# A four-layer gated cross-attention block on one core: key halves of the exponentials summed on VectorE ahead of the softmax denominators, and filler products moved

## The reference, cut to what matters

```
# layer 0 (as the attention inside its ffn block) and layer 3: causal, 16 heads of 16
scores = einsum('bhqd,bhkd->bhqk', qh, kh) / sqrt(16); scores = where(tril, scores, min)
attn = softmax(scores, axis=-1);  out = einsum('bhqk,bhkd->bhqd', attn, vh) @ Wout.T
# layer 1 ("latent"): 16 heads of 64, keys and values from the context, no mask
attn = softmax(q_h @ k_b^T);      out = (attn @ context_b) folded with the output weights
# layer 2 ("score attention", in the phase called mid): softmax over scores, times the scores' own rows,
# after a low-rank adapter with a top-8 gate, and before a top-2 router with capacity 64
```

## Time and profile before

| | us |
|---|---|
| median of 3 runs | 1128.38 |
| the 3 runs | 1126.38, 1134.92, 1128.38 |
| the profiled execution, its own time | 1119.47 |
| its span, first to last instruction | 1117.5 |
| mean granted TensorE clock in it | 0.951 of full |

### The profile page before, as it was taken

One profiled execution on the slowest core, in us unless ns is written; L12 is line 12 of the kernel. 1 busy time (PEld: TensorE's weight loads), 2 busy tenths in 40 slices (PEclk: granted clock), 3 DMA queues, 4 the chain that ended last, 5 costly groups with the idle time before them and its releaser, 6 DMA issues. The chain is left out here.

```text
span 1117.5 us, 23219 instructions
## 1 busy us (share of the span) xinstructions
PE 1004.8 (90%) x9278; PEld 821.0 (73%) x9278; DVE 715.8 (64%) x1737; ACT 483.4 (43%) x863; POOL 194.9 (17%) x167
## 2 busy tenths in 40 slices
PE   9979889879998899989899999885798899989998
PEld 5747677757787687878778887674696777778787
DVE  1567778867776675666666666657645677654644
ACT  1447777713334434435243333344342334334443
POOL 4100000020001132444330000033101000133342
PEclk9999999979999999999999999967798999899999
DMA  9500000000001122323000000010100000132232
GB/s 335 198 2 3 2 1 3 2 1 2 2 3 44 55 86 83 105 94 100 8 2 2 2 2 2 1 39 1 38 1 1 3 3 18 35 96 83 93 108 71
DMA packets 17706, 48.27 MB, mean 43 GB/s; under 512 B 3072, under 2 KB 5248, under 8 KB 17472
## 3 DMA queue, kind: packets, MB, share of 16 engines
q1 hardware_dynamic: 17600, 46.80, 12.9%
HBM read 45.61 MB, written 1.05 MB: 42 GB/s over the span
## 5 line engine op out<-in xcount | busy, mean ns | idle before, releaser
L1669 POOL TENSOR_TENSOR p_WML<-p_raw,p_WMH 128x768 fp32r<-128x768 f32 x56 | 103.7, 1852 | 155.5 <-ACT p_WMH L1786 150.0
L1822 ACT ACTIVATE p_AHI<-p_A 128x512 fp32r<-128x512 f32 x62 | 39.1, 631 | 142.0 <-DVE p_A L1909 142.0
L1349 ACT ACTIVATE p_E<-PS 128x768 f32<-128x768 f32 x64 | 51.6, 807 | 86.7 <-PE PS L1206 86.5
L1909 DVE TENSOR_TENSOR p_A<-p_A,PS 128x512 f32<-128x512 f32 x62 | 42.6, 687 | 62.0 <-PE PS L1717 61.1
L1913 DVE TENSOR_TENSOR p_ALO<-p_A,p_AHI 128x512 fp32r<-128x512 f32 x62 | 52.1, 841 | 44.0 <-ACT p_AHI L1822 44.0
L1453 DVE TENSOR_REDUCE p_mx<-PS 128x2 f32<-128x512 f32 x64 | 44.0, 688 | 53.6 <-PE PS L1170 53.4
L745 PE MATMUL PS<-p_FT,p_PTS 128*128 128x128 f32 x512 | 63.8, 278 | 12.0 <-DVE XNS L935 10.7
L745 PEld LDWEIGHTS PS<-p_FT,p_PTS 128*128 128x128 f32 x512 | 60.0, 192 | 17.3 <-DVE p_PTS L976 15.9
L83 PE MATMUL PS<-p_WMH,p_AHI 128*128 128x256 f32 x224 | 62.9, 281 | 1.6 <-DVE p_ALO L1913 1.4
L85 PE MATMUL PS<-p_WMH,p_ALO 128*128 128x256 f32 x224 | 62.6, 279 | 0.0
L84 PE MATMUL PS<-p_WML,p_AHI 128*128 128x256 f32 x224 | 62.6, 279 | 0.0
(11 more groups left out here) (523 smaller groups left out, 3269.9 us busy)
## 6 DMA issues: line engine op xcount, KB each, us to landing
p_raw<-in_moe SPq DMA_DIRECT2D x56, 448.0 KB, 3.3
p_fr<-in_fold SPq DMA_DIRECT2D x16, 480.0 KB, 4.6
p_raw<-in_wpack SPq DMA_DIRECT2D x8, 416.0 KB, 5.8
p_early_raw<-in_moe SPq DMA_DIRECT2D x6, 448.0 KB, 3.3
CP<-in_consts SPq DMA_DIRECT2D x1, 1725.0 KB, 9.1
XS<-in_x SPq DMA_DIRECT2D x1, 1024.0 KB, 14.4
W2R<-in_ffn SPq DMA_DIRECT2D x4, 256.0 KB, 3.4
p_W3R<-in_ffn SPq DMA_DIRECT2D x4, 256.0 KB, 3.3
```

What stands on the lines that cost most here:

```text
L1349: act.activation(E[:, n % 4], PS[:, ST:ST + 2, 0:384], ACT.Exp, scale=scale).then_inc(s["ex"], 1)
L1669: g.tensor_tensor(WML[:, n % RING, :], raw[:, i % RAW, 0:SEL], WMH[:, n % RING, 0:SEL].bitcast(F32), ALU.subtract).then_inc(s["w_lo"], 1)
L1909: v.tensor_tensor(A[:, b, :], A[:, b, :], PS[:, GS_BANK, :], ALU.mult).then_inc(s["ag"], 1)
```

## The change

Three edits.

1. In both small attentions DVE adds the two key halves of the exponentials of queries 128 to 255 (`key_sums(q)`, at odd steps, 512 elements a partition) into a new buffer ES; PE's products with ones take the queries 0 to 127 from E and 128 to 255 from ES, after a new wait on `es`. The products with the values stay.
2. In latent attention the same for all queries of the pairs 1 to 12 (`SUMMED`): two additions of 128x512 a pair on DVE, into HN's memory, and four products with ones instead of eight. The first addition waits for POOL's last use of HN (`mk`); ACT's writes of HN wait for the products of pair 12.
3. Fillers: 8 at the end of the latent phase, 6 in mid after `lora_turned(0)`, and the 16 in mid become 32 and wait for `neg` of half 1 (the negated maxima, which the exponentials need) instead of its second exponential.

```diff
@@ -1007,6 +1007,7 @@
                 E = ph.sb("E", [P, 4, 2, 384])
+                ES = ph.sb("ES", [P, 2, 2, P])
                 identr = ph.sb("identr", [P, P], F32R)
...
@@ -1232,11 +1233,16 @@
                                 lo, hi = (S, S + P) if kt else (0, S)
-                                for part in range(2):
-                                    for r in range(4):
-                                        left = OZ[:, 16 * p:16 * p + 32] if part else VZ[:, 2 * (j % 2) + kt, 4 * o + r, 16 * p:16 * p + 32]
-                                        m = pe.matmul(PS[32 * r:32 * r + 32, ND, part * S + kt * P:part * S + S], left, E[:, (2 * q + r // 2) % 4, r % 2, lo:hi],
-                                                      start=part == 0 and kt == 0 and p == 0, stop=part == 1 and kt == 1 and p == 1, skip_group_check=True)
+                                for r in range(4):
+                                    pe.matmul(PS[32 * r:32 * r + 32, ND, kt * P:S], VZ[:, 2 * (j % 2) + kt, 4 * o + r, 16 * p:16 * p + 32],
+                                              E[:, (2 * q + r // 2) % 4, r % 2, lo:hi], start=kt == 0 and p == 0, stop=False, skip_group_check=True)
+                            for qt in range(2):
+                                if qt:
+                                    pe.wait_ge(s["es"], q + 1)
+                                for r in range(4):
+                                    keys = ES[:, r // 2, r % 2, :] if qt else E[:, (2 * q + r // 2) % 4, r % 2, 0:P]
+                                    m = pe.matmul(PS[32 * r:32 * r + 32, ND, S + qt * P:S + qt * P + P], OZ[:, 16 * p:16 * p + 32], keys,
+                                                  start=False, stop=qt == 1 and p == 1, skip_group_check=True)
                             m.then_inc(s["pv"], 1)
...
@@ -1472,6 +1478,13 @@
 
+                        def key_sums(q):
+                            at = slice(2 * (q % 2), 2 * (q % 2) + 2)
+                            v.wait_ge(s["ex"], 2 * q + 2)
+                            if q:
+                                v.wait_ge(s["pv"], q)
+                            v.tensor_tensor(ES[:, :, :, :], E[:, at, :, P:S], E[:, at, :, S:S + P], ALU.add).then_inc(s["es"], 1)
+
                         def context_lo(u):
...
@@ -1573,6 +1586,8 @@
                                 context((n - 5) // 4)
+                            if n % 2:
+                                key_sums(n // 2)
                             if n % 4 == 2 and n >= 6:
...
@@ -1970,6 +1985,8 @@
                 E = ph.sb("E", [P, 4, 2, 2, S])
+                ES = HN[:, :, :].rearrange("p (a b) s -> p a b s", a=2)
+                SUMMED = range(1, 13)
                 mx = ph.sb("mx", [P, 2, 2, 2, 2])
...
@@ -2080,13 +2097,18 @@
                                 pe.wait_ge(s["tr_lo"], KC)
-                            for part in range(3):
+                            for part in range(2 if q in SUMMED else 3):
                                 o = PS[:, XY, part * S:part * S + S] if part < 2 else PS[:, DEN, 0:S]
                                 for kt in range(2):
                                     for i in range(4):
                                         left = CTN[:, 2 * j + kt, 32 * part:32 * part + 32] if part < 2 else ones1[:, 0:32]
                                         m = pe.matmul(o[32 * i:32 * i + 32, :], left, E[:, (2 * q + i // 2) % 4, i % 2, kt, :],
                                                       start=kt == 0, stop=kt == 1, skip_group_check=True)
+                            if q in SUMMED:
+                                pe.wait_ge(s["es"], 2 * (q - SUMMED[0]) + 2)
+                                for i in range(4):
+                                    m = pe.matmul(PS[32 * i:32 * i + 32, DEN, 0:S], ones1[:, 0:32], ES[:, i // 2, i % 2, :],
+                                                  start=True, stop=True, skip_group_check=True)
                             m.then_inc(s["pv"], 1)
...
@@ -2139,6 +2161,7 @@
                         m.then_inc(s["nx_mr"], 1)
+                        warm(pe, WARM["split"], bank=3)
 
...
@@ -2188,11 +2211,12 @@
                                 context_hi((n - 3) // 2)
-                            if 26 <= n < 26 + TT:
-                                if n == 26:
+                            if 0 <= n - 2 * SUMMED[-1] - 2 < TT:
+                                if n == 2 * SUMMED[-1] + 2:
+                                    act.wait_ge(s["pv"], SUMMED[-1] + 1)
                                     act.wait_ge(s["ln_nb"], 2)
                                     act.wait_ge(s["mk"], NT)
-                                t = n - 26
+                                t = n - 2 * SUMMED[-1] - 2
                                 act.activation(HN[:, t, :], XS[:, t, :], ACT.Identity, bias=nbias[:, t:t + 1], scale=rstds[:, t:t + 1]).then_inc(s["nx"], 1)
...
@@ -2228,6 +2252,15 @@
                             v.tensor_tensor(cols[:, :, :, 4:8], rows, cols[:, :, :, 0:4].bitcast(F32), ALU.subtract).then_inc(s["m_lo"], 1)
+
+                        def key_sums(q):
+                            v.wait_ge(s["ex"], 2 * q + 2)
+                            if q == SUMMED[0]:
+                                v.wait_ge(s["mk"], NT)
+                            else:
+                                v.wait_ge(s["pv"], q)
+                            for n in range(2 * q, 2 * q + 2):
+                                v.tensor_tensor(ES[:, n % 2], E[:, n % 4, :, 0, :], E[:, n % 4, :, 1, :], ALU.add).then_inc(s["es"], 1)
 
...
@@ -2278,6 +2311,8 @@
                                 context((n - 3) // 2)
+                            if n % 2 and n // 2 in SUMMED:
+                                key_sums(n // 2)
                             if n % 2 == 0 and n >= 4:
...
@@ -2414,6 +2449,7 @@
                         lora_turned(0)
+                        warm(pe, WARM["steps"], bank=MR[1])
                         pe.wait_ge(s[1]["t1_lo"], KC)
...
@@ -2425,8 +2461,8 @@
                         pe.wait_ge(s[0]["res"], TT)
-                        pe.wait_ge(s[1]["es"], 2)
-                        warm(pe, WARM["mid"], bank=BASE[0])
+                        pe.wait_ge(s[1]["neg"], 1)
+                        warm(pe, 2 * WARM["mid"], bank=BASE[0])
                         transposes(0, s[0]["n3"], s[0]["t3_done"], BASE[0])
```

More of the change, by code:

```diff
@@ L1000, in small_attention @@
                 pw_in = ph.sems("pw_in", PRE)
-                s = ph.sem(STATS + ROUTE + "pw_hi pw_lo nx hid pre ln_norm one sel_z sel l_eps l_rstd xn aux_pe aux_v tr_hi q_ab q_sum q_hi q_lo sc mxd m_hi m_lo mt mt_c "
+                s = ph.sem(STATS + ROUTE + "es pw_hi pw_lo nx hid pre ln_norm one sel_z sel l_eps l_rstd xn aux_pe aux_v tr_hi q_ab q_sum q_hi q_lo sc mxd m_hi m_lo mt mt_c "
                            "st ex pv rec ctx c_hi c_lo proj res sq rms_eps rms_rstd")
@@ L1958, in latent_attention @@
             with Phase() as ph:
-                s = ph.sem(STATS + "nx nx_t nx_hi nx_lo nx_mr ln_nb mk_in mkf mkg mk ln_norm tr_done tr_hi tr_lo sel_z sel kb_hi kb_lo qp q_hi q_lo sc mxd m_hi m_lo mt mt_c "
+                s = ph.sem(STATS + "es nx nx_t nx_hi nx_lo nx_mr ln_nb mk_in mkf mkg mk ln_norm tr_done tr_hi tr_lo sel_z sel kb_hi kb_lo qp q_hi q_lo sc mxd m_hi m_lo mt mt_c "
                            "st ex pv rec ctx c_hi c_lo proj res")
```

## The result

The changed kernel takes 1123.1 us in the median of 20 runs, the kernel before 1126.7 in 20 runs beside it: ratio 0.9968, 95% interval 0.9954 to 0.9982, or 3.6 us less. It is faster, by a third of a per cent; the forecast was 11.2 us. One of the 20 runs of the changed kernel took 3211.2 us and is left out of the ratio.

The account below looks back on a forecast made before the run. PE bounds the latent loop; in layer 0's attention PE and DVE are both near their limits. Terms -4.6 - 2.5 - 1.7 - 4.0 + 1.2 + 0.4 = -11.2 us from 1128.38 give 1117.2, range 1107 to 1128.

Parts of the forecast that it names:

- Small attentions: 16 pairs each: Both small attentions: ones over half the columns save PE 0.21 us a pair; taken -2.5 in layer 3, -1.7 in layer 0.
- The prediction's bound for each phase (+2.5): Each small attention: worst end +2.5 us, a quarter of the 16 additions, at 0.6, wholly on the path.
- Latent: Latent attention, 12 pairs: ones save PE 0.44 us a pair, DVE's additions nearly use its slack; taken -4.6 us.
- Mid: Mid phase: six fillers hold the clock, -4.0 us; 32 fillers instead of 16 cost +1.2 us.
- the six: Mid, six fillers in PE's 1.57 us gap: they hold the clock, so POOL's weights start earlier; -4.0 us.
- the 32: Mid, 32 fillers instead of 16 before the router: block starts earlier but ends later, transposes to 775.9; taken +1.2 us.
- End of latent: 8 fillers after PE's last product: PE ends 0.6 us behind POOL; +0.4 taken, ends +0.6 and -0.9.
- A: Rival: mid's clock falls all the same, so -4.0 is 0; -7.2 us, 1121; chance 0.20.
- B: Rival: DVE and ACT swallow the attentions' sums, half of -8.8 goes; -7 us, 1124 with A's half; chance 0.07.
- C: Rival, slower: latent additions cost 1.3 us each and DVE's chain sets the pace; +9 us, 1137; chance 0.07.
- D: Rival, more: the longer filler also carries the clock through mid's last router; 3.7 us more, 1113; chance 0.10.
- The rule on a DVE tensor_tensor held up by GpSimd: Small attentions: a sum meeting POOL's weight subtraction held up to about 1.2 us; one meeting a phase costs 2.4 us.

## Why the prediction was wrong

**The step that failed is "Small attentions: 16 pairs each"**, -2.5 and -1.7, where the version without them shows +4.5 for both (and the sums alone in the kernel before +3.3). That is 8.7 us off, more than the 7.6 by which the whole forecast was. The saving on PE was sized rightly (0.21 us a pair, 0.20 to 0.22 measured), and so was the addition: `key_sums` in the profile after,

```profile
L1486 DVE TENSOR_TENSOR p_ES<-p_E x32: 679/684/694, 257.7 to 975.1; 128x512 f32<-128x512 f32 x32
```

Two things were missed. First, in layer 3 I asked only whether DVE has free time and not what stands behind each sum: the evacuations of steps 3, 7, 15 and 23, each with a PE item already waiting. Four losses of 0.3 to 0.4 us and two of 0.1 to 0.2 eat the eight gains of 0.2 at full clock; behind the evacuations the same sums win 2.4 us by step 27. Second, I costed the shorter products at the upper clock level only. In layer 0, behind the wait of 1.90 us, the short products of pair 12 came with 13.6 us or more at the lower level in four of four profiles, the long ones in one of fourteen. The prediction's bound for each phase (+2.5) left this out: layer 0's attention alone is 4.6 us longer with the small sums (148.7 to 153.3). That pair 12's form matters is shown by the timed pair of kernels (0.9983 against 1.0029); by what means it keeps the clock down stays open, as the guess of a second idle time fails in the changed kernel's profile. In layer 3, 1.5 us of the loss are there without its sums too (135.7 against 134.2).

**Latent** was right: 0.43 to 0.44 us a pair for 12 pairs, 5.2 in all against 4.6 taken, while the timed runs of the latent sums alone show 2.9 (0.5 to 5.3), later phases being longer in their profile. The slack was as thin as worked out, but nothing was late. PE's timeline after, where the earlier trace rows had two groups of ones:

```profile
647.00 1.93 PE L2105 MATMUL PS<-p_E,CTN 128*32 128x256 f32 x32
648.75 0.61 PE L2110 MATMUL PS<-HN,ones 128*32 128x256 f32 x8
649.30 0.43 PE L2070 MATMUL PS<-p_identr,p_MM 128*128 128x128 f32 x2
```

and DVE's, where the earlier trace rows had no sums:

```profile
655.37 0.69 DVE L2271 TENSOR_TENSOR p_CT<-PS,p_rin 128x512 f32<-128x512 f32 x1
655.98 1.28 DVE L2263 TENSOR_TENSOR HN<-p_E 128x512 f32<-128x512 f32 x2
657.18 1.22 DVE L2241 TENSOR_REDUCE p_mx<-PS 128x4 f32<-128x1024 f32 x1
658.31 0.41 DVE L2237 TENSOR_TENSOR p_QL<-PS,p_QH 128x256 fp32r<-128x256 f32 x1
```

**Mid**: -4.0 for the six plus 1.2 for the 32 was the forecast, -2.8; measured -4.0. That the total comes near is in part luck: alone, the six gave 2.4 us, not 4.0, the eight at the end of latent gave 1.0 that wasn't counted, and 1.6 us appear only with all three together. The 32 cost 1.2 as taken, although the working for them comes to 1.9 (775.9 less 774.0). The chain was as written: the clock is held, the second router runs at full speed, and POOL's weights start earlier.

```profile
745.27 2.54 POOL L2372 TENSOR_TENSOR p_QL<-p_QR,p_QH 128x512 fp32r<-128x512 f32 x2 [8.47 <-ACT p_QH L2505]
747.77 5.03 POOL L2379 TENSOR_TENSOR W2L<-W2R,W2H 128x512 fp32r<-128x512 f32 x4
```

That is 18.7 us into mid, against 23.7 before. The run before the router, 8.35 us instead of 9.7:

```profile
762.24 8.35 PE L248 MATMUL PS<-onesb,identb 128*128 128x512 bf16 x32 [9.24 <-DVE p_sm L2614]
770.43 1.04 PE L2396 MATMUL PS<-CP,HN 128*128 128x128 f32 x8
773.79 1.20 PE L2396 MATMUL PS<-CP,p_HN 128*128 128x128 f32 x8 [2.33 <-DVE p_HN L2548]
```

It starts 6 us earlier and the second transposes wait 2.33 us for DVE, so part of the gain stops there. **End of latent**: +0.4, as predicted, with a gain of 1.0 in mid that the step bounded (-0.9) and didn't take.

**The rivals.** A fell (mid's clock holds). B comes near in time (1124) and not in its reason: latent swallowed nothing, and the small attentions went to the other side. C fell: 24 additions in latent at 0.68 us. D fell too: mid's last router still runs at the lower level. The rule on a DVE tensor_tensor held up by GpSimd (the Trainium skill, SBUF — State Buffer, section Who interferes with whom) had no chance to show: none of the 32 sums ran beside one of POOL's weight subtractions, and all lie between 0.679 and 0.694 us.

**The base.** The profile before was a quick one, 1119.47 us against a median of 1126.7; the second one took 1129.25. Between these two the same work in the setup, graph, first attention and last experts differs by 3.1, 1.7, 1.7 and 2.8 us, each time with more time at the lower clock.

## What to carry to other kernels

When work is put on an engine with free time, read what stands behind it in that engine's queue and who waits for that; placed one step later, behind the urgent entries, the same addition cost nothing up to step 27, and 2.7 us once where it then stood behind the router's chain. When work is taken from PE near one of its long waits, test each such place with timed runs, since the clock that goes with a shorter product can cost more than the product saves (5 us against 0.2 here), and single profiles of one kernel differ by several us. Here latent sums, the empty products, and small sums for pairs 0 to 11, with those of layer 3 behind the evacuations, make 0.9907 [0.9889, 0.9925], better than the kernel before and than the changed one. Without any small sums it is 0.9928 [0.9902, 0.9955], which these runs don't tell apart from it: that the small sums gain anything, even there, isn't shown.

## What the runs showed of the hardware

The same instructions at the same place met different clocks. In layer 3 the changed kernel's clock fell after a wait of 1.7 us in one profile, for 10.2 us, and in the next it did not; in layer 0 it fell around the wait of 1.90 us in 12 of 18 profiles, for 3.4 to 17.1 us, and not in the other six, where it fell some 8 us later for 3.4 us. The Trainium skill, TensorE: Matmul & The Clock Gate (The HAM clock gate), says that the chip's watch over TensorE runs free of the kernel, so that one kernel's clock changes at different places from run to run; the profiles agree with that, and the prediction should have given it a price: two profiles of one kernel lie 5 to 10 us apart (1119.47 and 1129.25 for the kernel before, 1135.13 and 1127.39 for the small sums alone, 1125.41 and 1120.37 for the changed kernel), nearly as much as this whole change was forecast to bring.
